# Cosine layer of a perceiver kernel: the norm and dot products of a tile issued one half tile later, alternating between the column halves of the array

## The reference

```python
def _L0_xattn_ref(visual_features, text_features, Wv, bv, Wt, bt):
    v = jnp.einsum('bsd,hd->bsh', visual_features, Wv) + bv      # 16 x 64 x 256
    t = jnp.einsum('bsd,hd->bsh', text_features, Wt) + bt        # 16 x 512 x 256
    dots = jnp.einsum('bih,bjh->bij', v, t)
    vn = jnp.linalg.norm(v, axis=-1)
    tn = jnp.linalg.norm(t, axis=-1)
    denom = jnp.maximum(vn[:, :, None] * tn[:, None, :], EPS)
    return dots / denom
...
x = x + _L0_xattn_ref(_layernorm(x, axis=-1), ctx_768, L0_xattn_Wv, L0_xattn_bv, L0_xattn_Wt, L0_xattn_bt)
```

## Time and profile before

| | |
|---|---|
| median of 3 runs | 2437.14 us (2428.78, 2437.14, 2438.85) |
| span of the profiled execution | 2436.2 us; it is not listed apart among the three times |
| cosine layer | PE work from about 14 us to 154 us of the span |
| one tile of it | 17.0 us: PE busy 17.00, ACT 11.94, DVE 10.76 |
| whole span | PE 83%, DVE 44%, ACT 38%, POOL 5% |

### The profile page before, as it was taken

One profiled execution on the slowest core, in us unless ns is written; L12 is line 12 of the kernel. 1 busy time (PEld: TensorE's weight loads), 2 busy tenths in 40 slices (PEclk: granted clock), 3 DMA queues, 4 the chain that ended last, 5 costly groups with the idle time before them and its releaser, 6 DMA issues. The chain is left out here.

```text
span 2436.2 us, 30012 instructions
## 1 busy us (share of the span) xinstructions
PE 2030.0 (83%) x9776; PEld 1440.0 (59%) x9776; DVE 1074.1 (44%) x2156; ACT 932.8 (38%) x1698; POOL 122.3 (5%) x138
## 2 busy tenths in 40 slices
PE   7979963999999399999999999999791345477999
PEld 5647762555555277778787877877571344433444
DVE  4656541010100252625335262533552577728993
ACT  5743310111111054544445454443442366605540
POOL 0000012000000200000000000000000000002220
PEclk9989955999999699999999999999895555579999
DMA  6400026678787310001100000100208644200000
GB/s 249 133 31 1 0 121 248 273 289 321 288 320 288 119 39 27 36 16 39 39 26 26 26 30 22 39 26 1 83 17 103 150 75 72 40 5 0 1 9 26
DMA packets 34038, 222.36 MB, mean 91 GB/s; under 512 B 5683, under 2 KB 5684, under 8 KB 25398
## 3 DMA queue, kind: packets, MB, share of 16 engines
q1 hardware_dynamic: 31414, 213.24, 26.8%
q0 software_dynamic: 2560, 8.39, 1.0%
HBM read 201.10 MB, written 20.51 MB: 91 GB/s over the span
## 5 line engine op out<-in xcount | busy, mean ns | idle before, releaser
L102 PE MATMUL PS<-cT,qs 128*128 128x512 f32 x1152 | 293.7, 400 | 7.0 <-ACT pb L1199 7.0
L1684 PE MATMUL PS<-cn,W1s 128*128 128x16 f32 x512 | 120.9, 377 | 186.1 <-DVE W1s L1626 186.1
L102 PE MATMUL PS<-pT,cN 128*128 128x512 f32 x1152 | 269.9, 392 | 1.7 <-DVE pT L1295 1.7
L897 PE MATMUL PS<-W,xgT 128*128 128x384 f32 x736 | 243.9, 490 | 1.4 <-ACT xgT L920 1.4
L102 PEld LDWEIGHTS PS<-cT,qs 128*128 128x128 f32 x1152 | 208.4, 188 | 57.3 <-issue 15.1
L102 PEld LDWEIGHTS PS<-pT,cN 128*128 128x128 f32 x1152 | 213.9, 188 | 45.1 <-DVE pT L1295 1.9
L1684 PEld LDWEIGHTS PS<-cn,W1s 128*128 128x128 f32 x512 | 114.0, 328 | 193.2 <-DVE W1s L1626 193.2
L897 PEld LDWEIGHTS PS<-W,xgT 128*128 128x128 f32 x736 | 140.9, 192 | 104.8 <-issue 12.5
L1194 ACT ACTIVATE qp<-PS 128x512 f32<-128x512 f32 x192 | 110.9, 596 | 196.4 <-PE PS L102 189.4
L102 PE MATMUL PS<-ws,xT 128*128 128x512 f32 x672 | 168.9, 410 | 11.0 <-DVE ws L1502 6.1
L1290 DVE TENSOR_REDUCE nmax<-PS 128x1 f32<-128x512 f32 x128 | 87.6, 684 | 160.5 <-PE PS L102 159.8
(11 more groups left out here) (220 smaller groups left out, 3071.2 us busy)
## 6 DMA issues: line engine op xcount, KB each, us to landing
W<-in_fc SPq DMA_DIRECT2D x23, 3072.0 KB, 12.6
W<-in_proj SPq DMA_DIRECT2D x23, 1536.0 KB, 6.7
vb<-scan_v SPq DMA_DIRECT2D x128, 128.0 KB
cT<-in_ctxT SPq DMA_DIRECT2D x16, 768.0 KB, 5.2
ct_in<-in_ctxT SPq DMA_DIRECT2D x16, 768.0 KB, 4.3
cn_in<-in_ctxN SPq DMA_DIRECT2D x16, 768.0 KB, 5.0
W<-in_w SPq DMA_DIRECT2D x2, 4096.0 KB, 83.4
routed_x<-zero SPq DMA_DIRECT2D x23, 256.0 KB, 5.4
```

Of the source, the lines that this page charges most:

```text
L102: mm = nc.tensor.matmul(out, lhs(m, s), rhs(n, s), start=(opens and (s, m, n) == terms[0]), stop=((s, m, n) == terms[-1]))
L897: mm = nc.tensor.matmul(ps[c][:, 0:HFE], xgT[:, k, :], fc[u][:, k, c * HFE:(c + 1) * HFE], start=(k == 0), stop=(k == DK - 1))
L1684: mm = nc.tensor.matmul(ps[u][:, col:col + B], rb[:, j % RB, k * P:(k + 1) * P], sel, start=True, stop=True)
```

## The change

The eight matmuls of step 6 leave the end of their tile. They are now `finish(i, p)`, and PE issues `finish(i-1)` in tile i between `project(i, 0)` and the transposes of v; `finish(7)` follows tile 7. Inside it the loops are turned: the two batches alternate, first for all norms, then for all dots, and all waits stand at its head. tT and sq get a second buffer, chosen by p. ACT's square root and DVE's four operations move in the same way into the next tile: on ACT between `project_out(0)` and `project_out(1)`, on DVE ahead of the copy of vT. The loop body holds two tiles now (tile 0 and tile 7 stand outside). The core of the diff:

```diff
-        tT = sbuf("tT1", [P, 2, 2, J])
-        sq = sbuf("sq1", [P, 2, 2, J])
+        tT = sbuf("tT1", [P, 2, 2, 2, J])
+        sq = sbuf("sq1", [P, 2, 2, 2, J])
...
+        def tiles(eng, tile, finish, turn=None):
+
+            tile(0, 0, True, False)
+            with eng.Fori(0, NT // 2 - 1) as i:
+                if turn is not None:
+                    turn(i)
+                tile(2 * i + 1, 1, False, False)
+                tile(2 * i + 2, 0, False, False)
+            if turn is not None:
+                turn(NT // 2 - 1)
+            tile(NT - 1, 1, False, True)
+            finish(NT - 1, 1)
...
+                def finish(i, p):
+                    pe.wait_ge(vt_sb, BASE + i + 1)
+                    pe.wait_ge(dots_read, BASE + i)
+                    pe.wait_ge(tn_sb, BASE + i)
+                    pe.wait_ge(t_sb, BASE + 4 * i + 4)
+                    pe.wait_ge(t_sq, BASE + 4 * i + 4)
+                    for m in range(2):
+                        for u in range(2):
+                            rows = slice(u * S, (u + 1) * S)
+                            mn = nc.tensor.matmul(psN[rows, :], ones[:, 0:S], sq[:, p, u, m, :],
+                                                  start=(m == 0), stop=(m == 1))
+                    mn.then_inc(n_mm, 1)
+                    for m in range(2):
+                        for u in range(2):
+                            rows = slice(u * S, (u + 1) * S)
+                            mm = nc.tensor.matmul(psD[rows, :], vT[:, m, rows], tT[:, p, u, m, :],
+                                                  start=(m == 0), stop=(m == 1))
+                    mm.then_inc(d_mm, 1)
...
                     project(i, 0)
+                    if not first:
+                        finish(i - 1, 1 - p)
                     pe.wait_ge(v_sb, BASE + i + 1)
...
                     project(i, 1)
                     if not last:
                         ln.tensor(pe, i + 1)
-                    pe.wait_ge(vt_sb, BASE + i + 1)
...
-                        for m in range(2):
-                            mn = nc.tensor.matmul(psN[rows, :], ones[:, 0:S], sq[:, u, m, :],
-                                                  start=(m == 0), stop=(m == 1))
...
                     project_out(0)
+                    if not first:
+                        finish(i - 1, 1 - p)
                     project_out(1)
                     if not last:
                         ln.scalar(act, i + 1, v_mm)
-                    act.wait_ge(n_mm, BASE + i + 1)
-                    act.wait_ge(dots_read, BASE + i)
-                    nc.scalar.activation(tn[:, :], psN[:, :], ACT.Sqrt).then_inc(tn_sb, 1)
```

More of the change, by code:

```diff
@@ L288, in tile @@
                     ch.link(nc.vector.tensor_tensor(x[:, i, :], x[:, i, :], cosv[:, :], ALU.add))
+                def tile(i, p, first, last):
+                    if not last:
+                        ln.vector_stats(ch, i + 1)
+                        ln.vector_norm(ve, i + 1)
+                        rest_c(i + 1, 0)
+                    if not first:
+                        finish(i - 1, 1 - p)
+                    ve.wait_ge(vt_mm, BASE + i + 1)
+                    ve.wait_ge(d_mm, BASE + i)
+                    nc.vector.tensor_copy(vT[:, :, :].rearrange("p m t -> p (m t)"),
+                                          psVT[:, 0:2 * P]).then_inc(vt_sb, 1)
+                    if not last:
+                        rest_c(i + 1, 1)
                 ve.wait_ge(w_hi, BASE + 1)
@@ L295, in _, with turn @@
                 ve.wait_ge(s_x2, BASE + 16)
[L296 to L301, removed]
+                def turn(i):
+                    if isinstance(i, int):
+                        assert ch.n == 12
+                        ch.again(i)
+                    else:
+                        ch.turn(i, 12)
+                tiles(ve, tile, finish, turn)
             @block.tensor
@@ L317, in project, with finish, tile @@
                                       lambda part, k: cs[part][:, u, k, :], CK).then_inc(t_mm, 1)
-                def tile(i, last):
+                def finish(i, p):
+                    pe.wait_ge(vt_sb, BASE + i + 1)
[15 more added lines that the diff above has]
+                    mm.then_inc(d_mm, 1)
+                def tile(i, p, first, last):
                     pe.wait_ge(ln.xT_ready, BASE + i + 1)
@@ L337, in tile @@
                         ln.tensor(pe, i + 1)
-                    pe.wait_ge(vt_sb, BASE + i + 1)
[L339 to L344, removed]
-                        for m in range(2):
-                            mn = nc.tensor.matmul(psN[rows, :], ones[:, 0:S], sq[:, u, m, :],
-                                                  start=(m == 0), stop=(m == 1))
[L348 to L357, removed]
+                tiles(pe, tile, finish)
             @block.scalar
@@ L367, in first_c, with finish, tile @@
                     nc.scalar.activation(cs[0][:, u], cT[:, u], ACT.Copy).then_inc(c_hi, 1)
-                def tile(i, last):
+                def finish(i, p):
+                    act.wait_ge(n_mm, BASE + i + 1)
+                    act.wait_ge(dots_read, BASE + i)
+                    nc.scalar.activation(tn[:, :], psN[:, :], ACT.Sqrt).then_inc(tn_sb, 1)
+                def tile(i, p, first, last):
                     act.wait_ge(v_mm, BASE + i + 1)
@@ L382, in project_out @@
                             act.wait_ge(t_mm, BASE + 4 * i + 2 * u + m + 1)
-                            act.wait_ge(d_mm, BASE + i)
-                            nc.scalar.activation(tT[:, u, m, :], psT[m][:, :], ACT.Identity,
+                            if not first:
+                                act.wait_ge(d_mm, BASE + i - 1)
+                            nc.scalar.activation(tT[:, p, u, m, :], psT[m][:, :], ACT.Identity,
                                                  bias=bt[:, m:m + 1]).then_inc(t_sb, 1)
@@ L387, in project_out @@
                             act.wait_ge(t_sb, BASE + 4 * i + 2 * u + m + 1)
-                            act.wait_ge(n_mm, BASE + i)
-                            nc.scalar.activation(sq[:, u, m, :], tT[:, u, m, :], ACT.Square).then_inc(t_sq, 1)
+                            if not first:
+                                act.wait_ge(n_mm, BASE + i - 1)
+                            nc.scalar.activation(sq[:, p, u, m, :], tT[:, p, u, m, :], ACT.Square).then_inc(t_sq, 1)
                         if not last:
@@ L404, in _ @@
                 first_c(0, 1)
-                with act.Fori(0, NT - 1) as i:
-                    tile(i, False)
-                tile(NT - 1, True)
+                tiles(act, tile, finish)
 def self_attention_layer(nc, a, e):
```

## The result

The changed kernel is slower: 2457.61 us, the median of four runs (2456.73 to 2467.77), against 2432.96 for the kernel before (four runs, 2425.83 to 2438.85, one more than the prediction had). The ratio is 1.0116, with a 95% interval of 1.0094 to 1.0137 (the quotient of the two medians alone is 1.0101). Of the two profiled executions, the spans are 2456.1 and 2436.2 us, 19.9 apart.

What follows compares the result with a forecast made beforehand. The cosine layer was taken as bound by PE, busy 17.00 of 17.00 us per tile. The move's +11.6 and the clock's +8.8 gave +20.4 on the 2436.2 span, 2456.6, and 0.9 more for the median: 2457.5 us, range 2445 to 2467.

Steps and rivals of the forecast that it cites:

- The wait for xT: Before the V product in tiles 0 to 6: PE waits 3.3 us for ACT's xT; V starts 3.93 us after project(i, 1).
- c: Time of the 16 norm and dots passes of one finish on PE: 3.6 us, bounds 3.5 and 7.0.
- finds its inputs ready: At finish(i-1): sq and tT are a half tile old, so the halves can run side by side, 8 slots, 3.44 us.
- The move without the clock: Tiles 0 to 6: V starts 1.95 us earlier each, the moved passes cost 3.6 each; 7 x (3.6 - 1.95) = +11.6 us.
- The clock: Behind the 3.3 us waits the granted clock falls to 0.50: +8.8 us, bounds 0 and 16.
- about 5.5 of 7: Number of the seven tiles in which the clock was expected to fall behind PE's wait, at 1.6 us each.
- The sum: Whole kernel: 11.6 + 8.8 = +20.4 us on the span of 2436.2, so 2456.6.
- Program order: Rival for finish's matmuls: passes start in program order, 3 us more, 2460; chance 0.04.
- The rival with nine slots: Passes in finish start in program order, nine slots instead of eight, 0.43 us more per tile; chance 0.04.
- the halves don't wait for each other's program order: PE's norms and dots: a norms pass of u = 1 starts ahead of an earlier-programmed dots pass; eight slots.
- DVE, tail, tile 7: DVE's vT some 7 us late but used half a tile later, the tail, tile 7's last norms: each costs nothing.

Runs made afterwards that it cites:

- xt_first: Changed kernel with ACT's xT moved behind the second tT, ahead of the two sq and the cast; 2430.19 us, ratio 0.9988 to the kernel before.
- by_batch: Changed kernel with finish's matmuls not alternating: norms and dots of u = 0, then those of u = 1; 2457.61 us, one run.
- filled: Changed kernel with three more matmuls per tile behind the transposes of xn, into a bank nothing reads; 2445.17 us, ratio 1.0049 to the kernel before.
- fill_one: Changed kernel with one more matmul per tile behind the transposes of xn, into a bank nothing reads; 2455.10 us, one run.
- xt_mid: Changed kernel with ACT's xT moved behind the two sq, ahead of the cast; 2452.98 us, ratio 1.0098 to the kernel before.
- both: Changed kernel with finish(i-1) between transposes of xn and next V product, and ACT's xT ahead of the two sq; 2422.44 us, ratio 0.9955 to the kernel before.

## Why the prediction was right, point by point

**The wait for xT.** Right in place and size. V starts 3.83 to 4.05 us behind the start of the transposes (3.93 said), PE waits 3.2 to 3.5 us, seven times (3.3 said). xt_first shows that ACT's order is the cause.

**c.** 3.58 measured, 3.6 said. Ready inputs were not the condition, as "finds its inputs ready" suggested; the alternation was (by_batch).

**The move without the clock.** The seven distances from the transposes to V add up to 27.2 us in the changed kernel and to 7 x 5.88 = 41.2 before, so with c the move costs 7 x 3.58 - (41.2 - 27.2) = +11.1, for +11.6 said. filled agrees: its layer is 14.9 us longer, with one low stretch of 6.8 us in it; at half speed that loses 3.4, which leaves 11.5.

**The clock.** The mechanism was right, its size too small: "about 5.5 of 7" at 1.6 gave 8.8. Seven fell. From the start of V to the first pass of `project` PE takes 3.97 to 4.24 us in the seven tiles, where it takes 2.55 at the full clock; together that is 11.3 us lost, 1.6 each, the price that I had taken. The term that was mis-sized is the count, and what lay under it, that a wait of a given length has a chance of its own each time. The runs show a pattern that repeats from tile to tile: 7 of 7 (twice), 7 of 7 with waits of 2.4 us, 6 of 7 with 1.9 us, but 2 of 7 in by_batch with 3.2 to 3.4 us. The rule of the Trainium skill that I set beside it (TensorE: Matmul & The Clock Gate, Loop structure matters more than you think: a loop with a long wait for a DMA in each turn runs its matmuls at the low clock in each) describes the changed kernel better than my count; by_batch, whose loop waits as long as the changed kernel's and mostly keeps its clock, doesn't follow it.

**The sum.** 11.1 + 11.3 = +22.4, and the layer shows 23.1, where I said 20.4. That the median came out at the 2457.5 predicted is luck: two errors went against each other. The prediction started from 2437.14, the median of three runs, and with the fourth run that median is 2432.96, 4.2 lower; by the medians the change costs 24.7 us, 4.3 more than the 20.4 of my sum. In the two profiled executions, 19.9 us apart, the layer's 23.1 is offset by the 3.4 us of the decayed attention, which no step of mine held. That part isn't the change's: cut at SP's first load of this layer and of the next, the layer takes 453.9 and 451.8 us in the two profiled executions of the changed kernel, and anything from 446.1 (by_batch) to 457.3 (before) in all eleven profiled executions, with the same work. Its waits differ. Changed, in that layer:

```profile
PE PS L1709 <- DVE W1s L1651: 183.3, 64, 48.5
ACT W1s L1676 <- DMA vb<-scan_v: 117.2, 7, 35.0
```

by_batch, the same:

```profile
PE PS L1708 <- DVE W1s L1650: 175.2, 64, 45.2
ACT W1s L1675 <- DMA vb<-scan_v: 108.6, 7, 31.3
```

PE waits there 8 us less, as ACT waits 9 us less for a DMA. The kernel before doesn't fit as simply: PE waits 186.1 us for the same there, yet ACT's wait for that DMA is listed with 108.4 us (5 times instead of 7). I take this layer for the source of much of the 13 us over which the four runs of the kernel before spread; that, and the DMA as the cause, was not tested.

**Program order.** The rival with nine slots is out: eight it is. The rule that I held against the rows (the same page of the Trainium skill, Part 3, The mechanism: matmuls start strictly in order) is contradicted here: in by_batch's timeline the first norm matmul of u = 1 starts at 83.75, and the second dots matmul of u = 0, ahead of it in the program, with its two passes at 84.60 and 85.03. For the same reason the sentence ahead of the prediction that every engine works strictly in the order written is too strong for PE. But my own reading, "the halves don't wait for each other's program order", is too strong as well: in by_batch four slots of each half run alone.

**DVE, tail, tile 7** at nothing: no wait of PE for them appears; before the last norms PE waits 1.9 us for sq, where the first four ran before.

**Open.** It stays open what makes the clock fall in each tile of one kernel and in few of another with like waits. One reading, not shown: it depends on when a wait comes, and not only on how long it is. In the changed kernel the low stretches start at 32.4, 52.9, 73.4, 93.9, 114.3, 134.8 and 155.3 us, evenly 20.5 apart, while the V products' starts are 20.1 to 20.5 apart; fill_one and xt_mid repeat at 20.5 us too. A fall thus comes with a tile of some 20.4 us, which by_batch has nearly (20.5) without one, and each next wait may meet the same condition, good or bad. No run moved the waits in time while leaving their length and spacing alone.

## What to carry to other kernels

Before moving work off the end of a loop turn, look for what it covered: here the matmuls that looked late hid another engine's chain for the next turn's first operand, and the chain's length behind the last shared event (3.8 us) against the work left between gave the first half of the loss (11.1 us). The low clock behind the waits gave the other (11.3 us). In this case waits of TensorE of 1.9 us and more in each turn were mostly followed by such a stretch (by_batch is the exception), so allow for a wait twice, once as itself and once as a low clock behind it, and fill it or shorten it: three useless matmuls per tile shortened this layer by 8.2 us. Shortening it by too little (xt_mid, 1.9 us left) brought 1.8 us. The matmuls on the two column halves paired when they alternated in the program (3.58 us); grouped by half they paired only in part (5.35 us), though their inputs were ready.

## What the runs showed of the hardware that was not expected

- 16 passes of 64 columns by 512 took 3.58 us alternating by pairs between the halves, and 5.35 us when eight of one half preceded eight of the other, with all inputs ready in both.
- Waits of 1.9 us in each tile were followed by 6.8 us at clock 0.50 in six tiles of seven, those of 2.4 and 3.3 us by 3.4 us at 0.50 in seven of seven; waits of 1.47, 0.9 and 0.7 us by none. The length of the stretch doesn't follow that of the wait: single waits of 3.2 (filled, tile 0), 3.3 (by_batch) and 2.85 us (both) had 6.8 us too.
- With waits of 3.2 to 3.5 us and some 20.5 us from one to the next, one kernel fell seven times of seven, in two executions, and another twice.
